# A decoder layer in one kernel: the scan's split moved between engines, and attention in another order of stages

## The chip, the core and the metric

The kernel runs on one core of a Trainium2 chip. The metric is the time of one execution on the device in microseconds (us). The core has TensorE (PE; matrix products), VectorE (DVE), ScalarE (ACT) and GpSimd (POOL), which work through their own instruction streams in order and meet only at semaphores, and SyncE (SP), which issues transfers.

## The reference, cut to what matters

```python
# x, ctx: (32, 128, 256); two of the stages that the change touches
x_dbl = einsum('bld,ed->ble', x, W_xproj)            # 64 columns dt_low, 16 B, 16 C
delta = softplus(dt_low @ W_dt.T + b_dt)
h = exp(delta_t * A) * h + (delta_t * x_t) * B_t     # scan over the 128 tokens, 16 states
x1 = layernorm(einsum(h, C_t) + x)
Q, K, V = x1 @ Wq.T, ctx @ Wk.T, ctx @ Wv.T          # 16 heads of 16
Q, K = layernorm(Q), layernorm(K)
o = softmax(Q K^T / 4) V @ Wo.T
x2 = layernorm(o + x1)                               # "the second norm"
gates = sigmoid(x2 @ Wg)
# then: 8 experts take their 1024 best rows each, GELU network, scatter-add, layernorm
```

## The kernel before

`build` runs five phases one after another: scan, attention, choice of rows, experts, final norm. The change touches the first two.

**Scan** (`scan_phase`). 32 sequences in 8 groups of 4 sequences (512 columns), two groups per turn of a loop. A group has 16 steps n, one for each state: TensorE spreads row n of B and of C over 128 partitions (`broadcast_b`, L211, `broadcast_c`, L216), VectorE multiplies (`drives`, L435) and scans (`scan`, L442), GpSimd multiplies by C (`outputs`, L514), TensorE adds the result up (`add_state`, L223), ScalarE makes the decays (L326) and copies C (L368). Within a group the next one is prepared: at n = 7 TensorE projects, at n = 8 ScalarE copies the result (`copy_low`, `high_part`), and B and C are split into three bf16 parts: VectorE subtracts the high part at n = 8 (`split`, L418), ScalarE rounds the rest twice at n = 9 (`middle_part`), VectorE subtracts again at n = 10 (`last_part`, L423). TensorE's `step_size` at n = 9 may overwrite the projection only when these have read it.

**Attention** (`attention_phase`). One sequence of 128 tokens at a time, software-pipelined by hand. Each engine has a function `step(q, live)` that lists its stages in a fixed order; `q.plus(n)` is the sequence n behind q, so that a step works at several sequences, each at another stage. `passes` runs the steps (opening and end unrolled, the middle as a loop of two steps). The order of an engine's work is only that list; where engines meet, `wait_ge` on a semaphore counts finished sequences. `since` is such a wait that is left out where its count is below one. The stages by their line: x1 copied (POOL L683), turned (PE L772), split in two parts (ACT L918, DVE L1005); context split (POOL L689, L691); projections of q and of k and v (PE L554 to L556, `products`); statistics of q, k (DVE L1010, L1014, L1020), inverse deviation (ACT L922, L925), normalising (DVE L1026, L1027), turn (PE L795), scaling (ACT L939, L942), bf16 and two-part copies (POOL L697 to L716); scores (PE L807), maxima (DVE L1034), turn of the maxima (PE L815, ACT L949), shifted scores and subtraction of the maximum (PE L825, L837), exponentials (ACT L955), mix of the values (PE L853), division (DVE L1039, L1042), mix in two parts (POOL L729, L733), output projection (PE), residual and its moments (DVE L1047, L1052, L1055), inverse deviation (ACT L960, L963), second norm (POOL L722), turn of x2 (PE L869, ACT L968), gates (PE L875, ACT L972, L975, DVE L1060).

In the order before, q is at its last stages (second norm, gates), q+1 at its mix, q+2 at scores, q+3 at the normalised q and k, q+4 at the projections.

## Time and profile before

| | |
|---|---|
| median of 3 runs | 1385.7 us (1383.73 to 1385.78) |
| profiled execution | 1390.1 us, its span 1388.3 us |
| busy in the span | PE 78%, DVE 72%, ACT 54%, POOL 57% |
| mean granted clock of TensorE | 0.929 of 2.4 GHz |
| scan | from 0 to about 522 us |
| attention | to about 884 us |
| choice, experts, final norm | to the end, not touched |

In the rows below, L with a number is a line of the kernel, times are in us from the span's start, "idle <-" says how long the engine stood before the instruction and what released it. A matmul row's duration reaches to the end of its result, so that the next one starts before it. PEclk is the clock that TensorE was granted, as a share of 2.4 GHz: 0.50 is 1.2 GHz.

### The profile page before, as it was taken

To read this page: it belongs to the slowest core of one execution; us is meant where nothing else is said; L and a number is where in the kernel's file an instruction comes from. 1 tells how busy PE (TensorE), PEld (TensorE's weight loads), DVE (VectorE), ACT (ScalarE), POOL (GpSimd) and SP (SyncE) were. 2 spreads that over 40 slices of the span, in tenths; PEclk is the share of its full clock that TensorE was granted. 3 is DMA by queue.
4 is the path that set the end of the run, shared out by engine and by line. 5 is a ranking of instruction groups with operands and counts; after the bars stand their busy time and mean duration, and the time that the engine had idled before them with its cause. 6 is when DMAs were issued, how large, how long until landed. Compare 5 with 4: busy or idle time off the path is not lost. (4 is left out here: it accounts for less than half of the span.)

```text
span 1388.3 us, 25930 instructions
## 1 busy us (share of the span) xinstructions
PE 1079.9 (78%) x8527; PEld 733.4 (53%) x8527; DVE 1000.8 (72%) x1898; ACT 751.8 (54%) x1601; POOL 794.1 (57%) x730
## 2 busy tenths in 40 slices
PE   5877778787777766888888888213999999999980
PEld 1332323233232224666666666103899989999970
DVE  2999999999999984787787776574455555555534
ACT  4666575666657624666667665202555555555433
POOL 2686776768677654777777775403144644454423
PEclk8999999999999997999999998556999999999995
DMA  3000000000000001111111100203134444434227
GB/s 108 16 16 1 16 0 15 1 15 15 0 1 0 1 0 33 37 35 42 38 34 43 38 31 33 77 0 110 55 66 108 97 104 72 107 84 79 42 22 254
DMA packets 43463, 64.01 MB, mean 46 GB/s; under 512 B 8288, under 2 KB 34592, under 8 KB 41248
## 3 DMA queue, kind: packets, MB, share of 16 engines
q1 hardware_dynamic: 31104, 46.11, 10.0%
q0 software_dynamic: 12288, 17.05, 7.5%
q8 instruction: 33, 0.54, 0.2%
q14 instruction: 38, 0.31, 0.1%
HBM read 42.00 MB, written 21.14 MB: 45 GB/s over the span
## 5 line engine op out<-in xcount | busy, mean ns | idle before, releaser
L514 POOL TENSOR_TENSOR scan_hc<-scan_state,scan_c_sb 128x1024 f32<-128x1024 f32 x128 | 305.4, 2391 | 142.8 <-DVE scan_state L442 132.9
L442 DVE TENSOR_TENSOR_SCAN scan_state<-scan_decay,scan_drive_ps 128x512 f32<-128x512 f32 x256 | 297.7, 1205 | 0.2
L223 PE MATMUL scan_y_ps<-scan_hc,all_ident 128*128 128x512 f32 x520 | 256.6, 617 | 3.1 <-POOL scan_hc L514 3.1
L1662 DVE TENSOR_TENSOR expert_hid_lo<-expert_hid,expert_hid_hi 128x512 fp32r<-128x512 f32 x128 | 88.6, 692 | 176.6 <-ACT expert_hid_hi L1646 163.4
L1559 POOL DMA_INDIRECT acc<-expert_rows,expert_lst x64 | 113.0, 1766 | 179.5 <-DVE expert_rows L1688 163.1
L1641 ACT ACTIVATE expert_hid<-expert_h_ps,expert_b 128x512 f32<-128x512 f32 x128 | 88.3, 690 | 199.0 <-PE expert_h_ps L556 175.8
L326 ACT ACTIVATE scan_decay<-scan_delta,scan_a_neg 128x508 f32<-128x508 f32 x256 | 169.6, 716 | 7.4 <-POOL scan_delta L496 7.2
L435 DVE TENSOR_TENSOR scan_drive_ps<-scan_dx,scan_b_ps 128x512 f32<-128x512 f32 x256 | 162.6, 681 | 14.3 <-POOL scan_dx L501 10.3
L368 ACT ACTIVATE scan_c_sb<-scan_c_ps 128x512 f32<-128x512 f32 x128 | 76.6, 599 | 138.7 <-PE scan_c_ps L216 129.6
L556 PE MATMUL expert_o_ps<-weights_w_hi,expert_hid_lo 128*128 128x256 f32 x512 | 143.2, 280 | 0.0
L223 PEld LDWEIGHTS scan_y_ps<-scan_hc,all_ident 128*128 128x128 f32 x520 | 99.8, 197 | 82.0 <-issue 72.7
L554 PE MATMUL expert_o_ps<-weights_w_hi,expert_hid_hi 128*128 128x256 f32 x512 | 143.1, 279 | 0.0
L555 PE MATMUL expert_o_ps<-weights_w_lo,expert_hid_hi 128*128 128x256 f32 x512 | 142.9, 279 | 0.0
L211 PE MATMUL scan_b_ps<-scan_bcs,scan_sel 96*128 96x512 bf16 x128 | 51.4, 401 | 114.5 <-DVE scan_drive_ps L435 114.5
L211 PEld LDWEIGHTS scan_b_ps<-scan_bcs,scan_sel 96*128 96x128 bf16 x128 | 12.4, 97 | 195.9 <-DVE scan_drive_ps L435 188.0
L554 PE MATMUL expert_h_ps<-expert_x_hi,weights_w_hi 128*128 128x512 f32 x256 | 106.2, 415 | 2.0 <-DVE expert_x_lo L1674 2.0
L556 PE MATMUL expert_h_ps<-expert_x_hi,weights_w_lo 128*128 128x512 f32 x256 | 101.9, 398 | 0.0
L555 PE MATMUL expert_h_ps<-expert_x_lo,weights_w_hi 128*128 128x512 f32 x256 | 101.8, 398 | 0.0
L555 PEld LDWEIGHTS expert_o_ps<-weights_w_lo,expert_hid_hi 128*128 128x128 f32 x512 | 96.1, 188 | 5.9
L554 PEld LDWEIGHTS expert_o_ps<-weights_w_hi,expert_hid_hi 128*128 128x128 f32 x512 | 96.0, 187 | 5.6
L556 PEld LDWEIGHTS expert_o_ps<-weights_w_hi,expert_hid_lo 128*128 128x128 f32 x512 | 96.1, 188 | 0.0
L1034 DVE TENSOR_REDUCE attn_top<-attn_s_ps 128x4 bf16<-128x512 f32 x128 | 84.0, 679 | 4.1 <-PE attn_s_ps L807 3.8
(221 smaller groups left out, 2452.9 us busy)
## 6 DMA issues: line engine op xcount, KB each, us to landing
weights_w<-w SPq DMA_DIRECT2D x16, 1024.0 KB
table<-all_row SPq DMA_DIRECT2D x32, 132.0 KB, 1.8
scan_xT<-xT SPq DMA_DIRECT2D x8, 512.0 KB, 4.0
attn_ctxT<-ctxT SPq DMA_DIRECT2D x32, 128.0 KB, 2.4
acc<-all_row SPq DMA_DIRECT2D x32, 128.0 KB, 1.7
final_a<-acc SPq DMA_DIRECT2D x8, 512.0 KB, 6.5
out<-final_o SPq DMA_DIRECT2D x8, 512.0 KB, 4.2
expert_b<-b SPq DMA_DIRECT2D x8, 128.0 KB, 3.0
```

The source lines that it names most:

```text
L223: last = pe.matmul(y_ps[k][:], ident[0][:], hc[:, n % RING, k, :], start=False, stop=(n == NS - 1))
L326: act.activation(decay[:, n % RING, k, :, 1:SEQ], delta[par][:, k, :, 1:SEQ], ACT.Exp, scale=a_neg[:, k, n:n + 1]).then_inc(decay_ready, 1)
L435: dve.tensor_tensor(drive_ps[k][:], dx[par][:, k, :], b_ps[:], ALU.mult).then_inc(drive_ready, 1)
L442: dve.tensor_tensor_scan(state[:, n % RING, k, :], decay[:, n % RING, k, :, :].rearrange("p b t -> p (b t)"), drive_ps[k][:], 0.0, ALU.mul ...
L514: pool.tensor_tensor(hc[:, n % RING, :, :], state[:, n % RING, :, :], c_sb[:, n % RING, :].unsqueeze(1).broadcast_to([P, KH, GT]), ALU.mul ...
L554: pe.matmul(out, a_hi, b_hi, start=start and n == 0, stop=False, skip_group_check=True)
L555: pe.matmul(out, a_hi, b_lo, start=False, stop=False, skip_group_check=True)
L556: last = pe.matmul(out, a_lo, b_hi, start=False, stop=stop and n == len(pairs) - 1, skip_group_check=True)
L1034: dve.tensor_reduce(top[:, j, 0:4], s_ps[j][:].rearrange("p (h k) -> p h k", k=P), AX.X, ALU.max).then_inc(m["top_done"], 1)
L1559: pool.indirect_dma_start(out=acc_dram, out_offset=bass.IndirectOffsetOnAxis(ap=lst[h.parity][:, n:n + 1], axis=0), in_=rows[h.part][:, t, ...
L1641: act.activation(hid[:, f % 2, :], h_ps[f % 2][:], ACT.Gelu, bias=b1[h.parity][:, f:f + 1]).then_inc(gelu_done, 1)
L1662: dve.tensor_tensor(hid_lo[:, f % RING_H, :], hid[:, f % 2, :], hid_hi[:, f % RING_H, :].bitcast(F32), ALU.subtract).then_inc(hid_ready, 1)
```

## The change

In the scan the split's two differences go from VectorE to GpSimd. GpSimd can't read the projection's bank, so ScalarE makes one more copy (`bc_full`, 64 x 512); the parts stand in other rows of `bcs` (the last one in rows 0 to 31), the middle part moves from n = 9 to n = 10, and `broadcast_b` waits for the last difference itself.

In the attention the second norm's scaling goes from GpSimd (subtract and multiply) to ScalarE (Identity with bias and scale), for which VectorE makes `o_shift` = -mean x deviation. All four lists have a new order. On TensorE the projections are those of q+3 instead of q+4, the turn of q and k and the turn of the maxima likewise of one sequence less, the output projection that of q; scores stay at q+2 and the mix at q+1, now behind the projections. The maxima are taken in the order 3, 2, 1, 0 and the exponentials 3, 0, 1, 2.

```diff
     def step_size(i, par):
         g = 2 * i + par
         pe.wait_ge(dt_copied, g + 1)
-        pe.wait_ge(bc_high, g + 1)
-        pe.wait_ge(bc_step, 4 * g + 1)
+        pe.wait_ge(bc_copied, g + 1)
         for k in range(KH):
             last = pe.matmul(m_ps[k][:], w_dt[:, k * P:(k + 1) * P], dt_low[:], start=True, stop=True)
...
-            pe.wait_ge(bcs_ready, g + 1)
...
         act.activation(bcs[par][:], m_ps[1][0:96, :], ACT.Copy).then_inc(bc_high, 1)
+        if not first:
+            act.wait_ge(bc_step, 4 * (g - 1) + 1)
+        act.activation(bc_full[:], m_ps[1][0:64, :], ACT.Copy).then_inc(bc_copied, 1)
 
     def softplus_parts(g, first=False):
...
-                if n == 9:
+                if n == 10:
                     middle_part(i + par, 1 - par)
-                if n == 10:
                     softplus_parts(g + 1)
                     softplus_exp(g + 1)
                 if n == 11:
...
 
+    def rest_part(i, par):
+        g = 2 * i + par
+        pool.wait_ge(bc_high, g + 1)
+        pool.wait_ge(bc_copied, g + 1)
+        pool.tensor_tensor(bc_rest[:], bc_full[:], bcs[par][0:64, :], ALU.subtract).then_inc(bc_step, 1)
+
+    def last_part(i, par):
+        g = 2 * i + par
+        pool.wait_ge(bc_step, 4 * g + 3)
+        pool.tensor_tensor(bcs[par][0:32, :], bc_rest[0:32, :], bc_mid[:], ALU.subtract).then_inc(bc_step, 1)
...
+                if n == 8:
+                    rest_part(i + par, 1 - par)
+                if n == 10:
+                    last_part(i + par, 1 - par)
                 if n == 11:
...
     def round_q(q):
+        pool.wait_ge(m["qk_ready"], q.b + 1)
+        since(pool, m["st_ready"], 4 * (q.b - 1))
+        pool.sem_inc(m["q_seen"], 1)
         pool.tensor_copy(q_hi[q.parity][:], qT[q.parity][:]).then_inc(m["q_high"], 1)
...
-        pool.wait_ge(m["o_rstd_ready"], q.b + 1)
-        since(pool, row_stored[q.parity], 32 * q.half)
-        pool.sem_inc(m["o_rstd_seen"], 1)
-        pool.tensor_scalar(row[q.parity][:, 0:D], res[:], o_mv[:, 0:1], o_rstd[:, 0:1], ALU.subtract,
-                           ALU.mult).then_inc(m["x2_ready"], 1)
 
...
 
     def step(q, live):
         if 2 in live:
+            round_k(q.plus(2))
+            rest_of_k(q.plus(2))
+        if 0 in live:
+            round_mix(q)
+            rest_of_mix(q)
+        if 2 in live:
             halve_k(q.plus(2))
-        if 0 in live:
-            normalise(q)
-        if 2 in live:
-            round_q(q.plus(2))
+        if 3 in live:
+            round_q(q.plus(3))
+        if 5 in live:
+            split_ctx(q.plus(5))
         if 4 in live:
             copy_x1(q.plus(4))
-        if 2 in live:
-            rest_of_q(q.plus(2))
-            rest_of_k(q.plus(2))
-        if 5 in live:
-            split_ctx(q.plus(5))
-        if 1 in live:
-            round_mix(q.plus(1))
-            rest_of_mix(q.plus(1))
         if 3 in live:
             halve_q(q.plus(3))
-            round_k(q.plus(3))
+            rest_of_q(q.plus(3))
 
...
         last.then_inc(m["g_ready"], 1)
 
     def step(q, live):
+        if 1 in live:
+            shifted_scores(q.plus(1), 0)
+            turn_top(q.plus(1))
+        if 3 in live:
+            project_kv(q.plus(3), 0)
+        if 1 in live:
+            shifted_scores(q.plus(1), 1)
+        if 2 in live:
+            turn_qk(q.plus(2))
+        if 3 in live:
+            turn_x1(q.plus(3))
+        if 1 in live:
+            subtract_top(q.plus(1))
+        if 3 in live:
+            project_kv(q.plus(3), 1)
+        if 0 in live:
+            project_out(q)
+        if 3 in live:
+            project_q(q.plus(3))
         if 2 in live:
             scores(q.plus(2))
         if 1 in live:
             mix_values(q.plus(1), 0)
         if 0 in live:
             turn_x2(q)
+            gates(q)
         if 1 in live:
             mix_values(q.plus(1), 1)
-        if 0 in live:
-            gates(q)
-        if 3 in live:
-            turn_qk(q.plus(3))
-        if 4 in live:
-            project_kv(q.plus(4), 0)
-        if 2 in live:
-            turn_top(q.plus(2))
-            shifted_scores(q.plus(2), 0)
-        if 4 in live:
-            turn_x1(q.plus(4))
-        if 2 in live:
-            shifted_scores(q.plus(2), 1)
-            subtract_top(q.plus(2))
-        if 4 in live:
-            project_kv(q.plus(4), 1)
-        if 1 in live:
-            project_out(q.plus(1))
-        if 4 in live:
-            project_q(q.plus(4))
 
     pe.wait_ge(const.ready, const.steps)
...
 
+    def normalise(q):
+        act.wait_ge(m["o_shift_ready"], q.b + 1)
+        since(act, row_stored[q.parity], 32 * q.half)
+        act.activation(row[q.parity][:, 0:D], res[:], ACT.Identity, bias=o_shift[:, 0:1], scale=o_rstd[:, 0:1]).then_inc(m["x2_ready"], 1)
+
...
         act.activation(g_den[:], g_exp[:], ACT.Copy, bias=1.0).then_inc(m["g_den_ready"], 1)
 
     def step(q, live):
+        if 2 in live:
+            inv_std_qk(q.plus(2))
+            copy_values(q.plus(2))
+            scale_qk(q.plus(2))
+        if 1 in live:
+            copy_top(q.plus(1))
+            exps(q.plus(1), 3)
+        if 3 in live:
+            high_of_x1(q.plus(3))
+        if 1 in live:
+            exps(q.plus(1), 0)
         if 0 in live:
             inv_std_o(q)
-        if 3 in live:
-            inv_std_qk(q.plus(3))
+        if 1 in live:
+            exps(q.plus(1), 1)
+        if 0 in live:
+            normalise(q)
+        if 1 in live:
+            exps(q.plus(1), 2)
         if 0 in live:
             copy_x2(q)
-        if 3 in live:
-            copy_values(q.plus(3))
-        if 0 in live:
             gate_exp(q)
-        if 2 in live:
-            copy_top(q.plus(2))
-        if 3 in live:
-            scale_qk(q.plus(3))
-        if 4 in live:
-            high_of_x1(q.plus(4))
-        if 2 in live:
-            for j in range(4):
-                exps(q.plus(2), j)
 
...
     def maximum(q, j):
...
         dve.bn_aggr(o_mv[:], o_stats[:]).then_inc(m["o_moments"], 1)
+
+    def shift_o(q):
+        dve.wait_ge(m["o_rstd_ready"], q.b + 1)
+        dve.scalar_tensor_tensor(o_shift[:], o_mv[:, 0:1], -1.0, o_rstd[:], ALU.mult, ALU.mult).then_inc(m["o_shift_ready"], 1)
 
...
         dve.reciprocal(gate_all[:, q.parity, :, ds(q.half, 1)].rearrange("p e o -> p (e o)"), g_den[:]).then_inc(m["gate_ready"], 1)
 
     def step(q, live):
-        if 0 in live:
-            moments_o(q)
-        if 3 in live:
-            statistics_q(q.plus(3))
         if 2 in live:
-            maximum(q.plus(2), 0)
-        if 3 in live:
-            moments(q.plus(3))
-        if 2 in live:
-            maximum(q.plus(2), 1)
+            maximum(q.plus(2), 2)
         if 3 in live:
             normalise_qk(q.plus(3))
         if 2 in live:
-            maximum(q.plus(2), 2)
-            maximum(q.plus(2), 3)
+            maximum(q.plus(2), 1)
+            maximum(q.plus(2), 0)
         if 1 in live:
             divide(q.plus(1))
         if 0 in live:
             sigmoid(q)
+        if 1 in live:
+            scale_mix(q.plus(1))
         if 4 in live:
             rest_of_x1(q.plus(4))
+        if 1 in live:
+            residual(q.plus(1))
+            statistics_o(q.plus(1))
+        if 4 in live:
+            statistics_q(q.plus(4))
             statistics_k(q.plus(4))
         if 1 in live:
-            residual(q.plus(1))
+            moments_o(q.plus(1))
+        if 4 in live:
```

TensorE, from the turn of q and k (attn_q_ps<-all_ident,attn_qkn) towards the subtraction of the maximum (xattn_pick), before and after:

```order
564 L795 MATMUL attn_q_ps<-all_ident,attn_qkn 128x128 x4
565 L554 MATMUL attn_kv_ps<-xattn_w_kv_hi,attn_ctx_hi 128x512
566 L555 MATMUL attn_kv_ps<-xattn_w_kv_lo,attn_ctx_hi 128x512
567 L556 MATMUL attn_kv_ps<-xattn_w_kv_hi,attn_ctx_lo 128x512
568 L815 MATMUL attn_turn_ps<-xattn_ident_bf,attn_top 128x128
569 L825 MATMUL attn_s_ps<-attn_q_hi,attn_k_hi 128x256 x4
570 L825 MATMUL attn_s_ps<-attn_q_lo,attn_k_hi 128x256 x4
571 L825 MATMUL attn_s_ps<-attn_q_hi,attn_k_lo 128x256 x4
572 L772 MATMUL attn_turn_ps<-all_ident,attn_x1b 128x128 x2
```

and after:

```order
571 L820 MATMUL attn_s_ps<-attn_q_hi,attn_k_hi 128x256 x4
572 L820 MATMUL attn_s_ps<-attn_q_lo,attn_k_hi 128x256 x4
573 L820 MATMUL attn_s_ps<-attn_q_hi,attn_k_lo 128x256 x4
574 L790 MATMUL attn_q_ps<-all_ident,attn_qkn 128x128 x4
575 L767 MATMUL attn_turn_ps<-all_ident,attn_x1b 128x128 x2
576 L832 MATMUL attn_s_ps<-attn_topT,xattn_pick 128x128 x16
577 L554 MATMUL attn_kv_ps<-xattn_w_kv_hi,attn_ctx_hi 128x512
578 L555 MATMUL attn_kv_ps<-xattn_w_kv_lo,attn_ctx_hi 128x512
579 L556 MATMUL attn_kv_ps<-xattn_w_kv_hi,attn_ctx_lo 128x512
580 L554 MATMUL attn_o_ps<-xattn_w_o_hi,attn_mixT_hi 128x256
```

Before, half of the k and v projection, the turn of the maxima and the first shifted scores stand between the turn of q and k and the turn of x1 (attn_x1b), and the subtraction is four rows further on. After, the turn of x1 and the subtraction follow at once.

GpSimd, one step of the loop before:

```order
165 L722 TENSOR_SCALAR all_row<-attn_res,attn_o_mv,attn_o_rstd 128x256
166 L708 CAST attn_q_hi<-attn_qT 128x512
167 L683 COPY attn_x1b<-front_x 128x256
168 L712 TENSOR_TENSOR attn_q_lo<-attn_qT,attn_q_hi 128x512
169 L716 TENSOR_TENSOR attn_k_lo<-attn_kT,attn_k_hi 128x256
170 L689 CAST attn_ctx_hi<-attn_ctxT 128x256
171 L691 TENSOR_TENSOR attn_ctx_lo<-attn_ctxT,attn_ctx_hi 128x256
172 L729 CAST attn_mixT_hi<-attn_mixT 128x256
173 L733 TENSOR_TENSOR attn_mixT_lo<-attn_mixT,attn_mixT_hi 128x256
174 L697 CAST attn_qb<-attn_qT 128x512
175 L705 CAST attn_k_hi<-attn_kT 128x256
```

and after, from the rounding of q (attn_q_hi):

```order
167 L712 CAST attn_q_hi<-attn_qT 128x512
168 L690 CAST attn_ctx_hi<-attn_ctxT 128x256
169 L692 TENSOR_TENSOR attn_ctx_lo<-attn_ctxT,attn_ctx_hi 128x256
170 L684 COPY attn_x1b<-front_x 128x256
171 L698 CAST attn_qb<-attn_qT 128x512
172 L716 TENSOR_TENSOR attn_q_lo<-attn_qT,attn_q_hi 128x512
173 L706 CAST attn_k_hi<-attn_kT 128x256
174 L720 TENSOR_TENSOR attn_k_lo<-attn_kT,attn_k_hi 128x256
175 L726 CAST attn_mixT_hi<-attn_mixT 128x256
176 L730 TENSOR_TENSOR attn_mixT_lo<-attn_mixT,attn_mixT_hi 128x256
177 L701 CAST attn_kb<-attn_kT 128x256
```

The scaling into all_row is gone. The rounding of q now opens a row of ten, in which the copy of x1 and, last but one, the two parts of the mix stand behind it; before, q's rounding stood behind the bf16 copy of the step before, and bf16 q and the first part of k behind the mix.

ScalarE, one step of the loop before, from the copy of x2:

```order
378 L968 ACTIVATE attn_x2T<-attn_turn_ps 128x256
379 L930 ACTIVATE attn_vz<-attn_kv_ps 128x8x2x16
380 L972 ACTIVATE attn_g_exp<-attn_turn_ps 128x8
381 L975 ACTIVATE attn_g_den<-attn_g_exp 128x8
382 L949 ACTIVATE attn_topT<-attn_turn_ps 128x128
383 L939 ACTIVATE attn_qT<-attn_q_ps,xattn_affine 128x128 x2
384 L942 ACTIVATE attn_kT<-attn_q_ps,xattn_norm 128x128
385 L939 ACTIVATE attn_qT<-attn_q_ps,xattn_affine 128x128 x2
386 L942 ACTIVATE attn_kT<-attn_q_ps,xattn_norm 128x128
387 L918 ACTIVATE attn_x1T_hi<-attn_turn_ps 128x256
388 L955 ACTIVATE attn_prob<-attn_s_ps 128x512 x4
389 L960 ACTIVATE attn_o_lnv<-attn_o_mv,xattn_eps 128x1
```

and after, from the copy of the maxima (attn_topT):

```order
406 L944 ACTIVATE attn_topT<-attn_turn_ps 128x128
407 L950 ACTIVATE attn_prob<-attn_s_ps 128x512
408 L913 ACTIVATE attn_x1T_hi<-attn_turn_ps 128x256
409 L950 ACTIVATE attn_prob<-attn_s_ps 128x512
410 L955 ACTIVATE attn_o_lnv<-attn_o_mv,xattn_eps 128x1
411 L958 ACTIVATE attn_o_rstd<-attn_o_lnv 128x1
412 L950 ACTIVATE attn_prob<-attn_s_ps 128x512
413 L963 ACTIVATE all_row<-attn_res,attn_o_shift,attn_o_rstd 128x256
414 L950 ACTIVATE attn_prob<-attn_s_ps 128x512
415 L968 ACTIVATE attn_x2T<-attn_turn_ps 128x256
416 L972 ACTIVATE attn_g_exp<-attn_turn_ps 128x8
417 L975 ACTIVATE attn_g_den<-attn_g_exp 128x8
```

Before, the four exponentials (attn_prob) stand together, with x2's inverse deviation behind them. After, the deviation and the scaling of x2 stand between them, and copy of x2 and gate exponential behind the last.

## Rows read from the trace of the kernel before

**Rows 1.** Windows: stretch, us; busy PE, PEld, DVE, ACT, POOL (xcount); PEclk, DMA.

```profile
400.00:500.00 100.00, 75.56 (x202) 30.01 (x201) 97.74 (x127) 60.29 (x104) 69.36 (x34) 0.98 0.00 1
600.00:700.00 100.00, 86.70 (x1478) 66.20 (x1468) 77.64 (x174) 64.97 (x195) 74.44 (x117) 1.00 0.11 37
```

**Rows 2.** Tile attn_res: ns min/median/max, first and last start, forms.

```profile
L1047 DVE TENSOR_TENSOR attn_res<-attn_o_ps,front_x x32: 424/425/427, 557.3 to 877.4; 128x256 f32<-128x256 f32 x32
```

**Rows 3.** Timeline of VectorE in the scan: start, us; [idle <-releaser].

```profile
179.55 2.33 DVE L442 TENSOR_TENSOR_SCAN scan_state<-scan_decay,scan_drive_ps 128x512 f32<-128x512 f32 x2
183.50 0.69 DVE L418 TENSOR_TENSOR scan_bc_rest<-scan_m_ps,scan_bcs 96x512 f32<-96x512 f32 x1 [1.62 <-ACT scan_bcs L300]
184.11 1.28 DVE L435 TENSOR_TENSOR scan_drive_ps<-scan_dx,scan_b_ps 128x512 f32<-128x512 f32 x2
...
191.07 0.68 DVE L423 TENSOR_TENSOR scan_bcs<-scan_bc_rest,scan_bc_mid 32x512 bf16<-32x512 f32 x1
192.01 1.29 DVE L435 TENSOR_TENSOR scan_drive_ps<-scan_dx,scan_b_ps 128x512 f32<-128x512 f32 x2 [0.26 <-DVE scan_bcs L423]
```

**Rows 4.** Timeline of TensorE in the same stretch.

```profile
182.19 0.38 PE L211 MATMUL scan_b_ps<-scan_bcs,scan_sel 96*128 96x512 bf16 x1
```

**Rows 5.** Groups by line: busy us, mean ns | idle before.

```profile
L712 POOL TENSOR_TENSOR attn_q_lo<-attn_qT,attn_q_hi 128x512 fp32r<-128x512 f32 x32 | 40.7, 1271 | 0.2
L722 POOL TENSOR_SCALAR all_row<-attn_res,attn_o_mv,attn_o_rstd 128x256 f32<-128x256 f32 x32 | 39.1, 1221 | 57.4 <-ACT attn_o_rstd L963 57.4
```

**Rows 6.** Timeline of all engines, one step of the steady attention.

```profile
703.63 0.30 ACT L922 ACTIVATE attn_qk_lnv<-attn_qk_mv,xattn_eps 128x2 f32<-128x2 f32 x1 [0.59 <-DVE attn_qk_mv L1021]
...
704.37 0.55 DVE L1026 TENSOR_SCALAR attn_qkn<-attn_kv_ps,attn_qk_mv,attn_qk_rstd 128x256 f32<-128x256 f32 x1 [0.20 <-ACT attn_qk_rstd L925]
...
705.18 0.43 PE L853 MATMUL attn_o_ps<-attn_prob,attn_vz 128*32 128x128 f32 x8
705.28 1.28 DVE L1034 TENSOR_REDUCE attn_top<-attn_s_ps 128x4 bf16<-128x512 f32 x2
705.29 0.39 ACT L968 ACTIVATE attn_x2T<-attn_turn_ps 128x256 f32<-128x256 f32 x1 [1.05 <-PE attn_turn_ps L869]
...
706.20 0.61 PE L875 MATMUL attn_turn_ps<-xattn_w_g,attn_x2T 128*128 128x8 f32 x4
...
706.66 0.63 PE L795 MATMUL attn_q_ps<-all_ident,attn_qkn 128*128 128x128 f32 x4
...
707.05 0.21 ACT L975 ACTIVATE attn_g_den<-attn_g_exp 128x8 f32<-128x8 f32 x1
...
708.36 0.81 ACT L939 ACTIVATE attn_qT<-attn_q_ps,xattn_affine 128x128 f32<-128x128 f32 x2
...
709.41 0.41 PE L837 MATMUL attn_s_ps<-attn_topT,xattn_pick 32*128 32x128 bf16 x16
...
710.08 0.49 ACT L942 ACTIVATE attn_kT<-attn_q_ps,xattn_norm 128x128 f32<-128x128 f32 x1
...
710.56 0.28 PE L554 MATMUL attn_o_ps<-xattn_w_o_hi,attn_mixT_hi 128*128 128x256 f32 x1
...
710.69 2.10 ACT L955 ACTIVATE attn_prob<-attn_s_ps 128x512 f32<-128x512 f32 x4
...
710.82 0.61 POOL L697 CAST attn_qb<-attn_qT 128x512 bf16<-128x512 f32 x1 [0.73 <-ACT attn_kT L942]
...
712.10 0.43 DVE L1052 BATCH_NORM_STATS2 attn_o_stats<-attn_res 128x6 f32<-128x256 f32 x1
```

**Rows 7.** Windows at the attention's first and last stretch, columns as rows 1.

```profile
528.00:532.00 4.00, 2.79 (x10) 1.97 (x9) 1.53 (x5) 0.66 (x2) 1.13 (x2) 0.61 0.20 57
860.00:864.00 4.00, 3.69 (x57) 3.00 (x53) 2.36 (x4) 0.67 (x3) 1.44 (x4) 0.50 0.00 0
```

**Rows 8.** Timeline of TensorE near the attention's end.

```profile
870.01 0.66 PE L853 MATMUL attn_o_ps<-attn_prob,attn_vz 128*32 128x128 f32 x8
...
871.88 1.02 PE L875 MATMUL attn_turn_ps<-xattn_w_g,attn_x2T 128*128 128x8 f32 x4
```

More of the change, by code:

```diff
@@ L465, in group @@
                             statistics(g)
-                        if n == 8 and not final:
-                            split(i + par, 1 - par)
-                        if n == 10 and not final:
-                            last_part(i + par, 1 - par)
                 dve.sem_inc(drive_ready, 1)
@@ L1082, in step @@
                         sigmoid(q)
+                    if 1 in live:
+                        scale_mix(q.plus(1))
                     if 4 in live:
                         rest_of_x1(q.plus(4))
+                    if 1 in live:
[3 more added lines that the diff above has]
+                        statistics_q(q.plus(4))
                         statistics_k(q.plus(4))
                     if 1 in live:
[L1087 removed]
+                        moments_o(q.plus(1))
+                    if 4 in live:
+                        moments(q.plus(4))
+                    if 1 in live:
+                        shift_o(q.plus(1))
+                    if 3 in live:
+                        maximum(q.plus(3), 3)
                 passes(dve, step)
```

36 lines of the change are left out of this document (15 added, 21 removed).

## The prediction

> **What bounds the kernel now.** I read the busy shares by stretch first. In the scan VectorE is busy 97.7 of 100 us, in the attention TensorE 86.7 of 100 while every other engine is under 78 [rows 1]. So the scan is bound by one engine, and each instruction taken off VectorE there is worth its time. The attention is bound by TensorE plus its waits. One sequence takes (877.4 - 557.3) / 31 = 10.33 us, from the first and the last start of the residual [rows 2]; TensorE is busy 0.867 x 10.33 = 8.95 us of it. A new order can therefore win at most some 1.4 us a sequence, 43 us over the 31 between, and can lose without any such limit. That is why the rest goes by one question: in the new order, which stage waits for which, and does the loop of waits close within one sequence?
>
> **The scan.** At n = 8 VectorE ends a scan at 179.55 + 2.33 = 181.9 and starts the next drives only at 184.11, since it waits 1.62 us for ScalarE's copy and then subtracts; at n = 10 the second subtraction puts the drives from 191.07 to 192.01 [rows 3]. Both go. Late next at n = 8 is TensorE, whose broadcast of B follows the projection and ends at 182.19 + 0.38 = 182.6 [rows 4]: the gain is 184.1 - 182.6 = 1.5 us. At n = 10 it is 0.95 us. Seven groups give 7 x 2.45 = 17 us. The differences now cost GpSimd two instructions a group. The nearest row, a subtraction of 512 columns, has 1.27 us [rows 5], so 2.5 us a group; GpSimd is idle 30 of 100 us there [rows 1] and the results are needed only at n = 15, so this costs nothing; if that cover were gone it would be 7 x 2.5 = 18 us. The extra copy on ScalarE (60 us busy of 100) also hides. ScalarE at n = 10 now waits for GpSimd's first difference, which stands behind the product of n = 8, two steps earlier; queued behind it are the softplus and the decays of n = 13, four steps' ring ahead of their use. I take -17 us, with ends 0 and -23 (all idle and busy time of both instructions, 7 x 3.3).
>
> **The attention, stage by stage.** The order of the code shows, for sequence numbers counted from the step's own s, this loop. Every "waits" is a semaphore wait in the code, or the place behind another stage in an engine's queue.
>
> 1. TensorE turns q and k of s+2. ScalarE then scales them (six instructions). GpSimd's rounding of q waits for that; behind it in its queue stand the split of the context, the copy of x1 for s+3, bf16 q, the rest of q, both parts of k, and only then both parts of the mix of s.
> 2. TensorE waits twice for that queue: its turn of x1 (s+3), which now stands right behind the turn of q and k, and its output projection of s. Subtract-the-maximum of s+1, and so every exponential, is behind the first.
> 3. Output projection and q projection, then on VectorE residual, statistics of x2, q and k, moments of x2; on ScalarE the logarithm and exponential of x2's variance; on VectorE the shift; on ScalarE the scaling of x2 and, behind it, the last exponential of s+1.
> 4. Scores of s+2 wait for that exponential. TensorE then does the first half of mix, the turn of x2, waits for ScalarE's copy, and the gates.
> 5. ScalarE's gate exponential, then behind it the inverse deviation of q and k of s+3; VectorE normalises q and k with it and only behind that takes the last two maxima of s+2; TensorE's shifted scores, first in its step, wait for these. Four stages later it turns q and k of s+3.
>
> The loop has closed, and it has gone on by exactly one sequence. So one sequence costs at least the sum of everything on it, and engines that could work beside each other stand in line. Off the loop are only TensorE's turn of x1, subtraction, second half of the kv projection and second half of the mix, GpSimd's bf16 k, and VectorE's reciprocal and other small work.
>
> **The sum of the loop.**
> - TensorE: 8.95 less the second half of mix (706.20 - 705.18 = 1.02), the subtraction with half of kv (710.56 - 709.41 = 1.15) and the turn of x1, about 0.35 (half of the turn's 0.63, with its issue). That is 6.4. At five places the end of the last matmul must now be awaited, where the next stage was issued before it (the gates last 0.61 us from 706.20, and the turn starts at 706.66): with 0.3 for these, 6.7 us [rows 6].
> - GpSimd: busy 74.4 of 100 us, or 7.69 a sequence [rows 1], less the scaling of x2 that goes away (1.22, [rows 5]) and bf16 k (0.40, an estimate from the 0.61 of bf16 q at 710.82, which is twice as large): 6.1, with its own waits 6.2 us.
> - ScalarE: scaling q and k 710.08 + 0.49 - 708.36 = 2.21; two pairs of logarithm and exponential, each 704.37 - 703.63 = 0.74 until VectorE starts on the result, of which 0.12 is the handing over, 1.2; one exponential of scores after the first such pair 0.48 (2.10 = 3 x 0.48 + 0.65), scaling x2 0.46 (an estimate: between this and the 0.39 of the copy of x2, at equal size), the last exponential 0.65; copy of x2 0.39; gate exponential and denominator 0.4 (from the gates' end, 706.20 + 0.61, to 707.05 + 0.21): 5.8 us [rows 6].
> - VectorE: two statistics and the moments before ScalarE may start, 0.9 (712.10 with 0.43 each); normalising q and k 705.28 - 704.37 = 0.91; two maxima 1.28: 3.1 us [rows 6].
> - Handing over, some fifteen times: 0.25 from ScalarE to GpSimd (710.08 + 0.49 to 710.82), 0.04 from TensorE to ScalarE (706.20 + 0.61 against its next, and 705.29), 0.12 to VectorE: 0.9 us in all [rows 6].
>
> 6.7 + 6.2 + 5.8 + 3.1 + 0.9 = 22.7 us, against 10.33 now, all at TensorE's full clock (2.4 GHz).
>
> **TensorE's clock.** It will not stay there. TensorE would work in five bursts of 1.5 to 2.5 us with idle time of 2.5, 5, 2.5 and 3.5 us between. In the attention's first stretch, with such bursts, the granted clock was 0.61 with TensorE busy 2.79 of 4 us, and in its last stretch 0.50 even at 3.69 of 4 us, after idle time had dropped it [rows 7]. At 1.2 GHz the half mix takes 871.88 - 870.01 = 1.87 instead of 1.02 and the gates 1.02 instead of 0.61 [rows 8]: factors of 1.83 and 1.67. By the smaller one, since most stages here are short and wait for their end, the 6.7 become 11.1 and the loop 27.1 us. The clock rises now and then in the longest burst, so I take 26.5 us. Both ends, 22.7 and 27.1, stay for the range.
>
> The Trainium skill has a rule on this (TensorE: Matmul & The Clock Gate, section "HAM oscillation — how this bites in real kernels"): where waits part short bursts of matmuls, each burst begins at the lower clock again. By it the loop would be the full 27.1 us and the kernel some 17 us above my time; the trace agrees so far, with its 0.50.
>
> **Ends of the phase.** Full steps stand between the first and the 30th output projection. The last two lack projections, turns and most of GpSimd's queue; by the same rows they are 14.9 and 14.4 us, and the one before is 3 to 4 us short of a full one: 29 x 26.5 + 25 = 794 us between first and last residual, in place of 320.1. The opening is three steps deep. Kv of s+1 now waits for the copy of the values of s, x1 for GpSimd's queue: the first residual comes some 24 us later after the phase's start. The new small shift on VectorE (0.16) is hidden behind an exponential on ScalarE; the added scaling on ScalarE is counted above; SyncE's loads and stores have over 10 us of slack in such a step. 794 - 320 + 24 = +498 us.
>
> **The sum.** Profiled span 1388.3 - 17 + 498 = 1869; the profile's span is 2.6 us above the median of the runs (1385.7), so 1867 us.
>
> **The rivals.**
> - *Full clock.* If the bursts keep the clock at 1.00, the loop is 22.7 us: 29 x 22.7 + 23 = 681, opening 20 us: 1386 - 17 + 361 + 20 = 1750 us. For it speaks that the steady steps keep 1.00 with TensorE idle 13 of 100 us [rows 1]; against it that it would be idle for more than half of the time. 13 in 100.
> - *Loop overheads.* Full loop at the low clock and 0.5 us a step for loop branches and register waits, in series now: 29 x 27.6 + 26 = 826: 1899 us. It is inside the range, 15 in 100.
> - *The loop is open at one place* (I misjudge one sequence number), most likely GpSimd's queue: then TensorE's turn, ScalarE's scaling and the copy of the maxima still stand between the turn of q and k and the subtraction, 2.3 us of idle TensorE a step, plus half of the rest: 12 to 17 us, or 1420 to 1580 us. 4 in 100.
> - *Faster.* The loop is no loop, engines are one step apart as they are now, and TensorE's stalls go: a step is TensorE's 8.95 us, 31 x 1.38 = 43 less, with the scan 1326 us. It decides from where no wait in a step needs another engine's work of the same step. Against it stand the eight waits above. 3 in 100.
> - *Scan gain lost* to GpSimd or TensorE: +17 us, beside any of these.
>
> **How the numbers follow.** Forecast (26 to 27 us a step, 1845 to 1885 us) 65 in 100, with overheads 15, full or mixed clock 13, open loop 4, faster 3. The range of 8 in 10 goes from 1770, in the mixed clocks, to 1905. Faster by over 0.2% (about what a measurement of this kernel can tell from no change) 0.03, within 0.2% 0.01, slower 0.96.
>
> **What would show it.** Right: the residual's starts are 25 to 28 us apart; TensorE's digits in the attention are 3 to 5 and its granted clock 0.5 to 0.7; its turn of x1 waits for GpSimd's x1 copy about 5 us and the output projection for mixT_lo 2 us or more; scores wait for the exponentials over 3 us, shifted scores for the maxima 2 us. In the scan no row of VectorE but drives, scans and statistics, and idle time under 1 us at n = 8. Wrong: starts of the residual under 20 us apart, or any of these waits absent.

## The result, and the profile after

| | before | after |
|---|---|---|
| median | 1385.7 us | 1885.5 us (1882.9 to 1886.4, 4 runs) |
| ratio | 1 | 1.360, 95% interval 1.358 to 1.362 |
| profiled span | 1388.3 us | 1884.5 us |
| mean granted clock | 0.929 | 0.757 |

The forecast was 1867 us, range 1770 to 1905. The spans differ by 496.2 us, and three places account for it: the scan's last instruction ends 20.3 us earlier, the opening of the attention takes 20.3 us more, and the 31 steps between the first and the last residual take 495.6 us more (0.6 us is left in the tail).

From the page of the kernel after, busy tenths of 40 slices and TensorE's granted clock in tenths:

```profile
PE   6788778887456565665556565556512999999991
PEclk8999999999765555555555555555556899999996
```

The attention reaches from slice 11 into slice 29, TensorE at 5 or 6 tenths and its mean granted clock at 5 or 6 tenths. The same stretch as in [rows 1], with the same columns, and the residual that answers [rows 2]:

```profile
600.00:700.00 100.00, 57.95 (x542) 41.02 (x538) 28.21 (x68) 27.51 (x78) 25.18 (x44) 0.57 0.04 14
```

```profile
L1052 DVE TENSOR_TENSOR attn_res<-attn_o_ps,front_x x32: 424/425/425, 557.3 to 1373.0; 128x256 f32<-128x256 f32 x32
```

No engine is busy all the time, and none has become the bound: a step of 27.3 us (alternating 27.2 and 27.4) has some 16 us of TensorE's work at half clock, 8 us of VectorE's, 7 of ScalarE's and 6 of GpSimd's. What the steps consist of shows in the waits of TensorE from 700 to 960 us, nine to ten steps (engine, what waits, for what: us in total, times, longest):

```profile
PE attn_turn_ps L767 <- POOL attn_x1b L684: 42.3, 9, 4.7
PE attn_s_ps L802 <- ACT attn_prob L950: 27.4, 9, 3.0
PE attn_s_ps L820 <- DVE attn_top L1037: 15.6, 10, 1.7
PE attn_o_ps L554 <- POOL attn_mixT_lo L730: 11.5, 9, 1.3
PE attn_turn_ps L870 <- ACT attn_x2T L968: 4.7, 10, 0.5
```

These are the five hand-overs to TensorE that the loop predicted. One turn of it, each row the point at which the chain passes to another engine (the timeline of all engines, rows between left out; in brackets the idle time and its releaser):

```profile
801.19 0.58 PE L554 MATMUL attn_o_ps<-xattn_w_o_hi,attn_mixT_hi 128*128 128x256 f32 x1 [1.27 <-POOL attn_mixT_lo L730]
...
805.03 0.29 ACT L955 ACTIVATE attn_o_lnv<-attn_o_mv,xattn_eps 128x1 f32<-128x1 f32 x1 [5.21 <-DVE attn_o_mv L1062]
...
807.16 0.61 PE L802 MATMUL attn_s_ps<-attn_kb,attn_qb 32*128 32x128 bf16 x16 [3.05 <-ACT attn_prob L950]
...
810.30 0.38 ACT L968 ACTIVATE attn_x2T<-attn_turn_ps 128x256 f32<-128x256 f32 x1 [3.28 <-PE attn_turn_ps L864]
810.73 1.02 PE L870 MATMUL attn_turn_ps<-xattn_w_g,attn_x2T 128*128 128x8 f32 x4 [0.47 <-ACT attn_x2T L968]
...
811.79 0.18 ACT L972 ACTIVATE attn_g_exp<-attn_turn_ps 128x8 f32<-128x8 f32 x1 [1.11 <-PE attn_turn_ps L870]
...
813.04 0.54 DVE L1029 TENSOR_SCALAR attn_qkn<-attn_kv_ps,attn_qk_mv,attn_qk_rstd 128x256 f32<-128x256 f32 x1 [3.86 <-ACT attn_qk_rstd L920]
...
815.36 0.59 PE L820 MATMUL attn_s_ps<-attn_q_hi,attn_k_hi 32*128 32x256 f32 x4 [1.74 <-DVE attn_top L1037]
...
822.33 0.62 POOL L712 CAST attn_q_hi<-attn_qT 128x512 fp32r<-128x512 f32 x1 [20.86 <-ACT attn_kT L937]
...
828.58 0.58 PE L554 MATMUL attn_o_ps<-xattn_w_o_hi,attn_mixT_hi 128*128 128x256 f32 x1 [1.28 <-POOL attn_mixT_lo L730]
```

From one output projection to the next it is 27.39 us, with no gap in the chain: GpSimd does nothing for 20.86 us of them and is still the one waited for twice.

The granted clock of 0.57 is a mean of the two levels. In the same step (columns as [rows 1]):

```profile
815.00:819.50 4.50, 4.14 (x31) 2.95 (x32) 2.35 (x5) 0.00 (x0) 0.00 (x0) 0.50 0.17 59
819.60:822.80 3.20, 0.21 (x2) 0.00 (x0) 0.00 (x0) 2.37 (x7) 0.47 (x1) 1.00 0.00 0
822.90:846.80 23.90, 16.13 (x151) 11.48 (x151) 8.13 (x19) 4.87 (x14) 5.73 (x11) 0.50 0.05 17
```

The clock does rise once in each steady step, right behind TensorE's densest burst (4.14 of 4.5 us). But by then TensorE is waiting for the copy of x1: it works for 0.21 of the 3.2 us at full clock, and all 16.13 us of work that follow run at 1.2 GHz.

In the scan, VectorE's rows at n = 8, which answer [rows 3]:

```profile
172.35 2.32 DVE L431 TENSOR_TENSOR_SCAN scan_state<-scan_decay,scan_drive_ps 128x512 f32<-128x512 f32 x2
175.52 1.29 DVE L424 TENSOR_TENSOR scan_drive_ps<-scan_dx,scan_b_ps 128x512 f32<-128x512 f32 x2 [0.85 <-PE scan_b_ps L211]
176.72 2.32 DVE L431 TENSOR_TENSOR_SCAN scan_state<-scan_decay,scan_drive_ps 128x512 f32<-128x512 f32 x2
```

Only scans and drives stand there, with 0.85 us of waiting for TensorE's broadcast.

### The profile page after: what moved, and what is told of

Read it like the earlier page. It is cut to its first block and busy times, and to the rows that moved or that the text cites. A ratio compares the mean times of both kernels' runs of the same rounds, so it can differ in the third digit from the quotient of the medians.

```text
span 1884.5 us, 25957 instructions
## 1 busy us (share of the span) xinstructions
PE 1295.4 (69%) x8527; PEld 870.7 (46%) x8527; DVE 994.9 (53%) x1914; ACT 768.8 (41%) x1641; POOL 765.0 (41%) x714
## 5 line engine op out<-in xcount | busy, mean ns | idle before, releaser
L508 POOL TENSOR_TENSOR scan_hc<-scan_state,scan_c_sb 128x1024 f32<-128x1024 f32 x128 | 301.0, 2357 | 112.2 <-DVE scan_state L431 92.4
L712 POOL CAST attn_q_hi<-attn_qT 128x512 fp32r<-128x512 f32 x32 | 19.7, 616 | 633.2 <-ACT attn_kT L937 633.2
L1008 DVE TENSOR_TENSOR attn_x1T_lo<-attn_turn_ps,attn_x1T_hi 128x256 fp32r<-128x256 f32 x32 | 13.6, 425 | 301.8 <-ACT attn_x1T_hi L913 301.8
L767 PE MATMUL attn_turn_ps<-all_ident,attn_x1b 128*128 128x128 f32 x64 | 22.0, 448 | 143.9 <-POOL attn_x1b L684 143.9
L934 ACT ACTIVATE attn_qT<-attn_q_ps,xattn_affine 128x128 f32<-128x128 f32 x128 | 51.8, 459 | 169.1 <-PE attn_q_ps L790 169.1
L950 ACT ACTIVATE attn_prob<-attn_s_ps 128x512 f32<-128x512 f32 x128 | 75.3, 592 | 108.1 <-PE attn_s_ps L832 108.1
```

Source lines behind the costliest of these rows:

```text
L508: pool.tensor_tensor(hc[:, n % RING, :, :], state[:, n % RING, :, :], c_sb[:, n % RING, :].unsqueeze(1).broadcast_to([P, KH, GT]), ALU.mul ...
```

## The experiments

Theory: a step is one closed chain through all four engines, and its length is the sum of what stands on it, at the clock that TensorE has. Rivals: one engine's amount of work decides; the lower clock alone decides; the scaling on ScalarE is at fault and not the order. Steps below are the means of the distances between residual starts in the steady part (the third to the 26th of 31); in the kernel before that is 10.3 us.

### The parts apart, in the old order

Scan alone (the new scan, the old attention):

> The kernel before with the scan's split of B and C alone in its new form; attention in its old order. Theory (the scan's gain is real and adds to whatever attention does): the trace after starts its last scan at 485.9 us, the one before at 506.2, so 20.3 us come in ahead of attention; here they stay, since the steady attention step of 10.33 us doesn't depend on when it starts: 1385.7 - 20.3 = 1365.4 us, last scan near 486, steps of 10.3 us. The prediction's own term was 17 us: 1368.7. Rival (attention can't start earlier, since the first residual stands at 557.3 us in both traces): the first residual stays near 557 and the time at 1385 to 1387 us.

Measured: 1366.7 us against 1384.5 beside it, ratio 0.987 (0.985 to 0.989). Its last scan starts at 486.0 us, the first residual moves from 557.3 to 535.0, the steps stay at 10.3 us. The gain is real, and this kernel is faster than both the one before and the one after. The medians give 17.8 us, the two traces 20 to 22. From the first scan's start to the last one's it is 459.0 us for 477.2, so 18.2 less; the first scan starts at 27.0 us for 29.0, which is not the split's doing: that start varies from 26.0 to 28.4 us in the traces with the new scan and is 27.1 us in the next kernel, which has the old one. Before's profiled execution is also 4.4 us above its median.

Scaling on ScalarE alone:

```
                     if 0 in live:          # ScalarE
                         inv_std_o(q)
+                        normalise(q)
                     if 3 in live:          # VectorE
                         statistics_q(q.plus(3))
+                    if 0 in live:
+                        shift_o(q)
```

> The kernel before with the second norm's scaling alone on ScalarE: it stands directly behind the two instructions of o_rstd, VectorE's shift of 0.16 us behind the statistics of q; scan and order of attention are the old ones. Theory (what hurts is the order, not the engine): in the steady step before, the row's 1.22 us on GpSimd start 0.30 us behind ScalarE's 0.20 us of o_rstd and the turn of x2 waits 1.08 us for them; on ScalarE the row is done after 0.16 + 0.59 us and two hand-overs of some 0.1 us, 0.4 to 0.6 us earlier, and GpSimd is rid of 1.22 of its 7.4 us a step: steps of 9.8 to 10.2 us instead of 10.33, 1370 to 1382 us. Rival (the scaling on ScalarE is itself a cause of the loss): ScalarE's logarithm for q and k comes 0.7 us later, the normalisation of q and k and VectorE's maxima behind it with it, and the step gets longer by 0.3 to 0.7 us: 1395 to 1408 us.

Measured: 1392.1 us, 7.5 slower (ratio 1.006, 1.004 to 1.008), the step 10.6 us. My theory, a gain, fell. The rival has the direction, with 1395 to 1408 us expected, so more than was measured.

```profile
702.81 0.26 DVE L1057 SCALAR_TENSOR_TENSOR attn_o_shift<-attn_o_mv,attn_o_rstd 128x1 f32<-128x1 f32 x1 [0.32 <-ACT attn_o_rstd L955]
703.19 0.60 ACT L960 ACTIVATE all_row<-attn_res,attn_o_shift,attn_o_rstd 128x256 f32<-128x256 f32 x1 [0.41 <-DVE attn_o_shift L1057]
704.02 0.43 PE L861 MATMUL attn_turn_ps<-all_ident,all_row 128*128 128x128 f32 x2 [1.27 <-ACT all_row L960]
```

The turn of x2 does come earlier, 2.07 us behind the moments instead of 2.60 (702.22 to 704.82 in the trace before). But VectorE stands 0.32 us for ScalarE's o_rstd and then shifts, and ScalarE's logarithm for q and k stands behind the row; the product with inv_sum that ends VectorE's part comes 6.56 us behind the moments instead of 6.04 (708.26 - 702.22), and the output projection now waits 0.5 us for mixT_lo. The shift's own duration (0.26 us here) is only part of these 0.5 us; the other part is the wait for its input, in the queue of an engine that others wait for. This is read from one trace; no run moved the shift alone.

Both together:

> Both of the above on the kernel before, so the whole change without its new order of attention. Theory (the order alone costs the time, the other two parts add up): the sum of the two runs beside it, 1350 to 1362 us, which would put the price of the order at more than 520 us. Rival (one of the other parts is only harmless in the old scan or the old clock): more than 10 us above the sum of the two.

Measured: 1373.9 us, ratio 0.992 (0.990 to 0.994), 7.2 above the scan alone: the two parts add, one down, one up (the sum of the two kernels' differences gives 1374.2). The 1350 to 1362 us expected rested on the gain that the scaling did not bring. What is left to the new order is 1885.5 - 1373.9 = 511.6 us, a little under the 520 expected.

### Opening the loop at its links

A control first: the copy of the maxima's turn moved ahead of the scaling of q and k on ScalarE, a stage that the chain of waits doesn't pass:

> The kernel after with one ScalarE stage moved: the copy of the maxima's turn stands ahead of the scaling of q and k instead of behind it, 4 to 5 us earlier. A control: in the loop as written down the last to come at the turn of x1 is GpSimd's copy of x1 (824.04 to 824.44 us in the step at 801 us), 2 us behind that copy (822.00 to 822.28). Theory: 0, within 4 us of 1885.5. Rival (any stage that comes earlier helps, since all engines wait for one another): 1 us or more a step, 1855 us or less.

Measured: 1886.1 us. Nothing, as expected.

GpSimd's queue in another order:

```
-round_k, rest_k (s+2); round_mix, rest_of_mix (s); halve_k (s+2); round_q (s+3); split_ctx; copy_x1; halve_q; rest_q
+round_k, rest_k, halve_k (s+2); round_mix, rest_of_mix (s+1); copy_x1; split_ctx; round_q (s+3); halve_q; rest_q
```

> The kernel after with GpSimd's stages in another order: the two halves of the mix, the context's split and the copy of x1 stand ahead of the rounding of q, whose wait for q and k ended last in the loop. None of them needs q or k, and their inputs are there 5 to 15 us earlier. Theory (loop, with GpSimd's 6.2 us in it): the turn of x1 no longer waits for GpSimd but for the ScalarE copy of the maxima's turn, and the output projection no longer for the mix; the step goes from 27.4 to 23.0 to 24.5 us (in the loop stay q's and k's scaling and the work of TensorE): -90 to -135 us, 1750 to 1795 us. Rival (the lower clock and TensorE's 16.4 us of work per step decide, GpSimd only follows): the step stays above 26.5 us, 1860 us or more.

Measured: 1754.1 us, 131 less and as the theory had it, the step 23.0 us, at a granted clock of 0.55 to 0.65. The same instructions on the same engines. The wait for mixT_lo is gone from the list and the turn of x1 waits for the other stage:

```profile
819.31 0.66 PE L770 MATMUL attn_turn_ps<-all_ident,attn_x1b 128*128 128x128 f32 x2 [2.63 <-ACT attn_topT L949]
```

That is the copy whose move gave nothing alone. So it was moved too, with the inverse deviation of q and k:

```
+copy_top (s+1)            # ahead of scale_qk (s+2), was behind it
+inv_std_qk (s+3)          # ahead of copy_x2 (s), was behind gate_exp (s)
```

> The kernel with GpSimd's mix, context and x1 ahead of the rounding of q (1754.1 us, 23.7 us a step), with two ScalarE stages moved too: the copy of the maxima's turn ahead of the scaling of q and k (in that kernel the turn of x1 waits 2.63 us for it), and the inverse deviation of q and k ahead of the copy of x2 instead of behind the gates' exponential (its moments are there 7 us earlier; the shifted scores wait 1.74 us for the maxima behind it). Theory (every link of the loop that is opened gives its wait back, also the one that gave nothing by itself): 2.6 and 1.7 us less, 19 to 20 us a step, 1610 to 1640 us. Rival A (moving the copy gave 0 before, so it gives 0 again): only the 1.7 us, 1700 us. Rival B (with the chain cut anywhere, the steps overlap at once): 12 us a step or less, 1400 us.

Measured: 1583.7 us, 170 less again and 26 below the range that the theory gave; the step is 17.1 us, where the two waits of 2.6 and 1.7 us leave 18.7. For the rest there is the clock, 0.77 to 0.79 now and 0.55 to 0.65 before; I didn't separate it, nor the two moved stages from each other. What TensorE still waits for is mostly this, 15 times from 700 to 960 us:

```profile
PE attn_s_ps L805 <- ACT attn_prob L955: 46.8, 15, 3.2
```

Six stages were moved over these two kernels, none was made cheaper, and 302 of the 512 us came back. So no engine's amount of work sets the step of 27.3 us. The 210 us that still separate this kernel from the old order (1373.9 us) were not opened by any run.

### Adding work on the loop and beside it

Two GpSimd copies into unused tiles, once ahead of the copy of x1, once where GpSimd idles:

> The kernel after with two additional GpSimd copies of 128x256 from a constant into unused tiles, ahead of the copy of x1, where the predicted loop of waits runs through GpSimd (0.40 us each, some 0.5 with the step between them). Theory (a step is one closed chain, so everything put on it lengthens it): +0.9 to 1.1 us in each of some 31 steps, +28 to +34 us: 1913 to 1920 us. Rival A (the step is set by TensorE at its lower clock, 60% busy, or by another engine's own work): nothing, 1884 to 1888 us. Rival B (GpSimd's own amount of work matters): the same as in the run beside it.

> The same two additional copies on the same engine of the kernel after, but ahead of the bf16 copy of k, where GpSimd has up to 20 us left before its next wait ends. Theory of the loop: GpSimd's output parts of the mix are done by then and nothing on the chain waits for this copy of k (scores come 6 us later): 0 to +3 us, 1883 to 1889 us. Rival B (amount of GpSimd work): +28 to +34 us as in the run beside it.

Measured: 1889.6 and 1887.3 us. The second is as expected. The first is a miss: 4 us where 28 to 34 were expected, and the step is still 27.3 us. From its trace, GpSimd's copies and TensorE's turn of x1, then the scores and the first matmuls of the mix:

```profile
799.73 0.74 POOL L687 CAST attn_spare<-xattn_w_q_hi 128x256 fp32r<-128x256 f32 x2
800.42 0.40 POOL L689 COPY attn_x1b<-front_x 128x256 f32 x1
...
800.87 0.69 PE L772 MATMUL attn_turn_ps<-all_ident,attn_x1b 128*128 128x128 f32 x2 [5.43 <-POOL attn_x1b L689]
...
810.93 0.40 PE L807 MATMUL attn_s_ps<-attn_kb,attn_qb 32*128 32x128 bf16 x16 [3.05 <-ACT attn_prob L955]
811.26 0.43 PE L853 MATMUL attn_o_ps<-attn_prob,attn_vz 128*32 128x128 f32 x8
```

The copies took 0.69 us, not 1.0, and all of it arrived at the turn of x1: 5.4 us of waiting for 4.7. But the scores ran in 0.40 us, where they take 0.61 in the kernel after, and the mix's first quarter in 0.43 for 0.66. From the scores to the turn of x2 it is 1.64 us instead of 2.41. TensorE had the full clock there:

```profile
808.60:811.80 3.20, 0.87 (x36) 0.80 (x40) 0.92 (x6) 1.96 (x5) 0.00 (x0) 1.00 0.00 0
812.00:822.00 10.00, 7.79 (x82) 5.24 (x72) 5.05 (x10) 1.65 (x6) 0.00 (x0) 0.50 0.07 26
822.20:825.50 3.30, 0.43 (x4) 0.19 (x2) 0.00 (x0) 2.37 (x7) 0.36 (x1) 1.00 0.00 0
```

Every second step has such an additional stretch at full clock, with scores and mix in it, and takes 27.1 us; the others take 27.5. The mean is the 27.3 us of the kernel after, at a granted clock of 0.60 for 0.57. The clock gave back what the copies took. So this pair alone doesn't show what is on the loop.

### The clock by itself

Additional matmuls, whose result nobody reads, ahead of two of TensorE's waits; the second kernel has the two copies as well. These kernels, and the one with every wait filled, also have the maxima's copy ahead, which by itself gave nothing (1886.1 us):

```
+def fill(count):
+    for _ in range(count):
+        pe.matmul(turn_ps[:, KH * P:2 * KH * P], q_w_hi[:, 0, 0:P], q_w_hi[:, 0, :], start=True, stop=True, ...)
...
+                        pe.wait_ge(m["top_ready"], q.b + 2)
+                        fill(20)                  # ahead of turn_x1
...
+                        fill(12)                  # ahead of scores
```

> The kernel with the maxima's copy ahead (1886.1 us), plus additional matmuls of 128x256 whose result nobody reads, where TensorE would stand still: 20 ahead of the turn of x1 (wait 4.68 us), 12 ahead of the scores (wait 3.05 us); 0.21 us each at the lower clock, 0.115 at full clock, so they fit the waits at either. They are there to see what the clock alone costs. Theory (part of the loop is TensorE's 11.1 us at 1.2 GHz instead of 6.7 at 2.4): the granted clock of the steady stretch rises from 0.57 to 0.9 or more, the step falls from 27.4 to 22.7 to 24 us, 105 to 145 us less: 1740 to 1785 us; the waits for GpSimd and ScalarE stay, hidden in the additional matmuls or not. Rival A (the clock isn't tied to what TensorE does here): 0.57 still, 1884 to 1895 us. Rival B (the loop is TensorE's own amount of work, not a chain of hand-overs): the step gets longer by what the matmuls take, 2.5 us or more, 1960 us.

> The same with the two additional GpSimd copies ahead of the copy of x1 as well, which added 0.7 us to TensorE's wait in each step of the earlier run, while scores and mix then ran at full clock and gave 0.8 us back. Theory (the copies are on the loop, and only the clock hid them): with the clock the same in both, +0.7 us in some 31 steps, 18 to 26 us above the run beside it. Rival (the copies are in the shadow of something else): within 4 us of the run beside it.

Measured: 1827.8 and 1853.3 us, steps of 25.2 and 26.1 us. The windows 700 to 800 us of both, the clock third from the end:

```profile
700.00:800.00 100.00, 66.89 (x720) 54.91 (x720) 32.53 (x76) 29.58 (x84) 25.16 (x44) 0.79 0.05 15
```

```profile
700.00:800.00 100.00, 70.28 (x696) 57.15 (x692) 29.79 (x72) 27.98 (x79) 27.91 (x52) 0.74 0.05 16
```

The clock rose to 0.8 only, so the first gained 58 us and not 105 or more: the waits for mixT_lo and for the maxima had no additional matmuls, the one for the copy of x1 still lasted 1.9 us behind its own, and behind the wait for mixT_lo (2.41 us at 811.23) matmuls of 0.28 us took 0.41 again. The copies cost 25.5 us, as the loop wants, but with the clock 0.05 lower not all of it is their own; some 20 us are 0.69 times 29. The kernel with them was run twice, at 1849.8 and 1856.8 us, so the figure is good to a few us.

So every wait was filled (30, 14, 18 and 14 matmuls):

> As the kernel with 20 and 12 additional matmuls, where the granted clock rose from 0.57 to 0.81 only and three waits stayed empty (1.9 us for x1b, 2.4 for mixT_lo, 2.2 for the maxima): now 30 ahead of the turn of x1, 14 ahead of the output projection, 18 ahead of the scores, 14 ahead of the shifted scores. Theory (what is left of the lower clock comes from the waits that are left): the granted clock of the steady stretch is 0.95 or more, the step comes to the sum of the loop at full clock, 22.7 us, against 25.0 with the fewer matmuls: 1750 to 1775 us. If the clock is full and the step is still above 24, my sum of the loop's other engines is too small. Rival (additional matmuls don't raise the clock further and outlast the waits at 0.21 us each): 1830 us or more.

Measured: 1753.5 us. The same window:

```profile
700.00:800.00 100.00, 83.36 (x1000) 71.56 (x988) 36.43 (x84) 32.65 (x94) 26.24 (x47) 1.00 0.06 19
```

```profile
801.07 0.44 PE L770 MATMUL attn_turn_ps<-all_ident,attn_x1b 128*128 128x128 f32 x2 [1.13 <-POOL attn_x1b L684]
...
824.00 0.44 PE L770 MATMUL attn_turn_ps<-all_ident,attn_x1b 128*128 128x128 f32 x2 [1.07 <-POOL attn_x1b L684]
```

The clock is 1.00 and the step alternates between 22.6 and 22.9 us, where the sum of the loop at full clock said 22.7. TensorE still waits at all four places behind its additional work. The lower clock therefore costs 27.3 - 22.7 = 4.6 us a step and 132 us of the kernel; the other 380 of the order's 512 us are the chain itself and some 20 us of its opening, which a full clock leaves standing.

### The order without the scaling

> The kernel after with the second norm's scaling back on GpSimd (its old instruction of 1.22 us, ahead of the rounding of q, where GpSimd waits 20.9 us), without VectorE's shift: so the new order and the new scan alone. In the old order the scaling on ScalarE cost 7.2 us (with the new scan). Theory: in the new order its 0.49 us stand between the second and the third of the exponentials that the scores wait for, so without it the loop is 0.5 us shorter, and GpSimd's row is done 2.7 us before its turn: -13 to -17 us, 1868 to 1873 us. Rival A (the scaling is in a shadow in this order): 1884 to 1887 us. Rival B (the shorter wait ahead of the scores takes the clock's gain or loss with it, as the two copies did): up to 15 us on either side of that, 1855 or 1885 us.

Measured: 1865.1 us, 20.3 less, 3 us beyond the range of the theory; the step 26.6 us (25.8 to 27.1). The scores wait 2.56 us instead of 3.05, as worked out, which is 0.5 of the 0.7 us a step. The kernel's windows of 100 us show 0.53 to 0.57, no better clock on average, but where the full clock falls is different:

```profile
743.70:770.60 26.90, 16.18 (x152) 11.32 (x152) 7.89 (x18) 6.86 (x20) 7.51 (x12) 0.50 0.05 15
771.90:775.10 3.20, 0.79 (x32) 0.72 (x36) 1.25 (x6) 1.47 (x4) 1.22 (x1) 1.00 0.00 0
```

The first line is a step of 27.1 us without any full clock. In the next one, of 25.8 us, the full clock covers the scores and the start of the mix. Steps of the second kind come every few steps, where the kernel after has none before its end; they can account for the remaining 5 us, though no run separates the two. The scaling on ScalarE costs in both orders, 7 us in the old and 20 in the new; beside 498 us between this kernel and the scan alone it is small.

## Why the prediction was right

The range held, the mechanism was as worked out, and the time was 18.5 us low: the span is missed by 15 us, and the rest comes from the span of the kernel after lying 1 us below its median, where I took over the 2.6 us above of the kernel before. By its steps:

- **Scan, -17 us.** Right. The traces give -20.3: 18.3 between the first and the last scan, which is 2.6 us in each of seven groups for my 2.45, and 2.0 ahead of the first scan (it starts at 27.0 instead of 29.0 us). The 2.0 us are no gain of the change, since the start of the first scan varies as much between kernels with the same scan. By medians of the kernel with this part alone it is -17.8. GpSimd's two differences take 1.15 us each, estimated at 1.27, and hide. VectorE's 0.85 us at n = 8 is TensorE's broadcast, the one named as late next.
- **The loop.** Right in each of its five links, as the waits and the closed chain of 27.39 us show. Three were opened by experiment (the copy of x1, mixT_lo, the maxima) and the one at the scores shortened by 0.5 us; the one at the copy of x2 stands on the trace alone. Its terms at the lower clock, from the chain above, hand-overs included:

| | foretold | measured |
|---|---|---|
| TensorE | 11.1 | 2.96 + 3.14 + 1.06 + 4.57 = 11.7 |
| GpSimd | 6.2 | 6.25 |
| ScalarE | 5.8 | 2.13 + 0.43 + 1.25 + 2.40 = 6.2 |
| VectorE | 3.1 | 0.88 + 2.32 = 3.2 |
| handing over | 0.9 | in the others |
| sum | 27.1 | 27.4 |

- **The clock.** This is the term that was mis-sized. I took 26.5 us, on the ground that the clock would rise now and then in the longest burst. It rose once in every steady step, but behind the longest burst, where TensorE has 0.21 us of work in 3.2 us (819.60 to 822.80 above). The rows of the chain are at 1.2 GHz (scores 0.61, half a mix 1.85, gates 1.02), and the step is 27.3. 29 x 0.8 = 23 us too little; the scan and the start of the first one gave 3 us more than foretold and the opening cost 4 us less, which by luck offsets part of it and leaves the 15 us by which the spans miss. The rows of before had said 0.50 [rows 7]; I talked the number down against them. The Trainium skill's rule (TensorE: Matmul & The Clock Gate, section "HAM oscillation — how this bites in real kernels"), that each burst behind a wait begins at the lower clock, told there of waits for transfers, gave 17 us more and was right for this kernel. In every second step of the kernel with the two copies, though, the scores and half of the first mix ran at full clock behind the same wait of 3.05 us.
- **The factor 1.67** for TensorE's part held: 4.4 us foretold between the clocks, 4.6 measured with the waits filled.
- **Ends of the phase.** The last two steps were foretold as 14.9 and 14.4 us and are 14.7 and 14.8. The opening was foretold as 24 us more and is 20.3.
- **The rivals.** Full clock, 22.7 us a step and 1750 us: not what happened, but with the clock restored by additional matmuls the kernel takes 1753.5. The loop does not open anywhere by itself, and nothing was gained but the scan. *Loop overheads* (27.6 us a step) would also give nearly the measured step, but the chain closes at 27.39 us without such a term.
- **The scaling of x2** stood in the sum with its duration alone. In the new order that holds for the wait: the shift runs beside an exponential, and without both the scores wait 0.5 us less, 0.2 us a step short of what came back. What failed is the expectation for the old order, where I let the shift cost its 0.16 us and not the wait in front of it.
- **What would show it.** The turn of x1 waits 4.7 us (foretold 5), the scores 3.05 (over 3), the shifted scores 1.7 (2); the output projection waits 1.3 where I said 2 or more, as TensorE gets there later at half clock. TensorE's digits are 5 and 6, not 3 to 5: a busy share counts the longer matmuls of the lower clock.

## What to carry to other kernels

In a kernel whose engines hand one another work, write down for each wait which sequence's work it is for, and follow them once around: if the walk comes back to where it began, one sequence later, the step is the sum of all of it, and no engine's busy share will tell. Such a loop opens link by link: the move of the maxima's copy gave nothing alone, and behind the other moves it was one of two that gave 170 us. The price of an instruction in a shared queue is its own duration and the wait that it brings in front of it; and a probe that lengthens a wait of TensorE has to be read with the granted clock beside it.

## What the hardware showed that was not expected

- The granted clock turned a cost into nothing: 0.7 us more waiting in one place of the step, and in every second step TensorE ran its scores at 2.4 GHz ten microseconds later, steps of 27.3 us on the mean with and without. A mean granted clock doesn't tell this: 0.57 and 0.60 look alike, but what counts is whether TensorE has work in the stretches at full clock, 0.21 of 3.2 us in the one kernel and 0.87 of 3.2 us in the additional stretch of the other. Why the additional stretch comes at all is open.
- 76 additional matmuls in each step, on an engine that was waiting, made the kernel 132 us faster. It is no way to build it, since the old order takes 1386 us without them, but it prices the clock.
- A GpSimd subtraction of 512 columns takes 1.15 us on 64 partitions and 1.15 on 32, against 1.27 on 128 [rows 5].
